# Linear attention of layer 0: one wait of TensorE moved behind the products with the carried state

## The reference, cut to what matters

```python
xn = _layernorm(x)
qkv = xn @ Wqkv + bqkv                     # split into q, k, v and 16 heads
# for every block of tokens, with a state S carried from block to block:
scores  = einsum('bhid,bhjd->bhij', qb, kb) * intra_decay
o_intra = einsum('bhij,bhjd->bhid', scores, vb)
o_inter = einsum('bhid,bhde->bhie', qb * q_decay, S)
S       = blk_decay * S + einsum('bhjd,bhje->bhde', kb * k_decay, vb)
o       = o_intra + o_inter
s = o @ Wout + bout
```

## Time and profile before

| what | value |
|---|---|
| time, median of 3 runs | 3000.16 us (2997.89 to 3001.02) |
| time of the profiled execution | 2999.55 us |
| its span, first to last instruction | 2997.8 us |
| granted TensorE clock, mean over the span | 0.984 |
| the attention of layer 0 in the span | about 0 to 574 us |
| share of the span in which PE is busy | 95% |

### The profile page before, as it was taken

The page is one execution under the profiler, slowest core; times in us unless marked ns, Lnnn a source line. Parts: engine busy times, 40 slices in busy tenths (PEclk is TensorE's granted clock), DMA queues, the critical chain, the costliest instruction groups (busy, mean ns, idle before and its releaser), DMA issues. The chain is left out here.

```text
span 2997.8 us, 54358 instructions
## 1 busy us (share of the span) xinstructions
PE 2848.9 (95%) x19392; PEld 2011.7 (67%) x19392; DVE 1857.0 (62%) x2721; ACT 1291.0 (43%) x2021; POOL 1416.7 (47%) x1003
## 2 busy tenths in 40 slices
PE   6999999799999997799999999999999789999999
PEld 5878787688888886455555555555555368888887
DVE  5656766577777764666666666666666744444444
ACT  3221111266666663355555555555555522222222
POOL 2003555122333222377777777777777732222222
PEclk9999999999999998799999999999999999999999
DMA  3221211122232224122222222222222332222221
GB/s 127 88 61 49 65 61 53 36 71 85 84 105 84 84 90 160 58 71 71 71 71 72 71 71 71 71 71 71 72 78 77 121 127 85 85 89 86 91 84 49
DMA packets 124567, 238.99 MB, mean 80 GB/s; under 512 B 13440, under 2 KB 48384, under 8 KB 124416
## 3 DMA queue, kind: packets, MB, share of 16 engines
q1 hardware_dynamic: 120896, 235.32, 23.2%
q10 hardware_dynamic: 3520, 1.46, 0.2%
HBM read 178.02 MB, written 58.72 MB: 79 GB/s over the span
## 5 line engine op out<-in xcount | busy, mean ns | idle before, releaser
L1330 DVE TENSOR_REDUCE l_attn_maxima<-l_attn_ps_max 128x2 f32<-128x1024 f32 x502 | 613.6, 1222 | 234.2 <-PE l_attn_ps_max L1455 230.2
L1301 POOL TENSOR_TENSOR l_attn_summed<-l_attn_summed,stage 128x1024 f32<-128x1024 f32 x248 | 586.0, 2397 | 52.9 <-ACT stage L1239 52.9
L1239 ACT ACTIVATE stage<-l_attn_ps_sc 128x1024 f32<-128x1024 f32 x512 | 497.8, 1029 | 157.3 <-PE l_attn_ps_sc L1443 136.0
L1301 POOL TENSOR_TENSOR l_attn_summed<-stage 128x1024 f32<-128x1024 f32 x124 | 293.4, 2388 | 240.1 <-ACT stage L1239 240.1
L1702 POOL TENSOR_TENSOR l_ffn_ht_lo<-stage,l_ffn_ht_hi 128x512 fp32r<-128x512 f32 x88 | 114.0, 1296 | 413.9 <-ACT l_ffn_ht_hi L1723 413.9
L62 PE MATMUL l_attn_ps_prep<-l_w_tile,l_x_tiles 128*128 (+1 forms) x1440 | 287.1, 348 | 6.3 <-DVE l_attn_qk_lo L1324 2.0
L62 PEld LDWEIGHTS l_attn_ps_prep<-l_w_tile,l_x_tiles 128*128 128x128 f32 x1440 | 248.9, 190 | 39.3 <-issue 29.4
L1465 PE MATMUL l_attn_ps_y<-stage,l_attn_v 128*32 128x512 f32 x2048 | 273.6, 606 | 1.1 <-ACT stage L1239 1.1
L71 PE MATMUL l_ffn_ps_fc<-l_w_tile 128*128 128x512 f32 x1024 | 268.1, 405 | 6.7 <-DVE l_w_tile L865 5.0
L71 PEld LDWEIGHTS l_ffn_ps_fc<-l_w_tile 128*128 128x128 f32 x1024 | 184.6, 190 | 41.7 <-issue 5.5
L71 PE MATMUL l_ffn_ps_out<-l_ffn_t_proj,l_ffn_ht_hi 128*128 128x512 f32 x512 | 206.9, 404 | 0.0
(11 more groups left out here) (270 smaller groups left out, 6328.6 us busy)
## 6 DMA issues: line engine op xcount, KB each, us to landing
l_x_tiles<-xt_chunks SPq DMA_DIRECT2D x160, 512.0 KB, 3.7
xt_chunks<-l_w_tile SPq DMA_DIRECT2D x32, 512.0 KB, 4.7
l_attn_xin<-in_x SPq DMA_DIRECT2D x32, 256.0 KB, 4.3
l_attn_piece<-in_w_fcT SPq DMA_DIRECT2D x16, 512.0 KB, 4.3
s<-l_attn_s_sb SPq DMA_DIRECT2D x32, 256.0 KB, 2.2
l_attn_piece<-in_w_projT SPq DMA_DIRECT2D x16, 512.0 KB, 3.9
l_ffn_xa<-in_x SPq DMA_DIRECT2D x32, 256.0 KB, 2.7
l_ffn_xb<-in_x SPq DMA_DIRECT2D x32, 256.0 KB, 2.9
```

What stands on the lines that cost most here:

```text
L1239: act.activation(probs[kt % RING][:, hs, :], ps_sc[:, hs, :], ACT.Exp, scale=ATT_SCALE).then_inc(exp_done, 1)
L1301: pool.tensor_tensor(total[:, hs, :], old[:, hs, :], probs[kt % RING][:, hs, :], ALU.add).then_inc(added, 1)
L1330: dve.tensor_reduce(maxima[b][:, j, PAIR * hp:PAIR * hp + PAIR, half:half + 1], pair, AX.X, ALU.max).then_inc(max_read, 1)
```

## The change

The wait for `masked_ready` is taken from ahead of the four products of the carried state and put behind them, just ahead of the products that read `masked`. No instruction is added or removed.

```diff
                     need(pe, zeroed, 1)
                     need(pe, state_ready, c)
                     need(pe, ot_lo_ready, c)
-                    need(pe, masked_ready, HPG * c + HPG)
                     for g in range(GROUPS):
                         pe.matmul(ps_o[:, g, :], state[q][:, g, :], q_dec[q][:, g, :], start=(g == 0), stop=False,
                                   skip_group_check=True)
+                    need(pe, masked_ready, HPG * c + HPG)
                     for g in range(GROUPS):
                         for h in range(HPG):
                             v = 2 * DIM + P * g + HD * h
```

## The result

The changed kernel takes 2989.39 us (median of 8 runs, 2987.75 to 2994.77), the one before 3000.48 (8 runs, 2997.89 to 3003.15): ratio 0.9963, 95% interval 0.9953 to 0.9972, so 8 to 14 us less. Forecast were 2991.7 us and a range of 2989 to 2997; the time lies 0.4 us inside the lower end of that range. Its profiled execution took 2989.26 us, with a span of 2987.5 us.

A forecast was written before the change was run, and what follows sets the result against it. PE, busy 95% of the span, was taken as the bound. Gains of 7.4 (ticks 15 to 29) + 1.1 (tick 1) + 0 (new wait's cost) = 8.5 us, off 3000.16, gave 2991.7 us; range 2989 to 2997.

The forecast's parts named there:

- The loss is 0.47 to 0.50 us in 15 ticks: Attention of layer 0, ticks 15 to 29: PE's stall ahead of L533 and slower L533 vanish, gaining 7.4 us in all.
- the idle time in brackets: PE's waits ahead of L533 in the profile, 6.1 us in 16 waits; said to understate the stall.
- The new wait is met 0.67 us early and costs nothing: Ahead of L538 in ticks 15 to 29, masked banks are ready 0.67 us before PE arrives; cost taken as 0.
- the rule on weight loads: At the L533 to L538 seam: TensorE may pull weight loads ahead, so a wait there could keep later loads back.
- second rival: The 15 late ticks stay at 17.1 us because something else ends last; only tick 1 gains: 2999.1 us, chance 0.12.
- first rival: The new wait costs 0.10 us in each of 32 ticks, so 5.3 us are gained: 2994.9 us, chance 0.10.
- DVE's idle time falls to 0.3 and DVE does not become the bound: Late ticks: DVE's wait for the q projection shrinks from 0.80 us to 0.3; DVE still waits for PE.
- the slower one: The wait keeps PE from holding L538's short load and matmul pairs ready: some 3007 to 3075 us, chance 0.06.
- Tick 1 gains 1.06: L533 runs inside PE's 2.70 us gap, so L538 starts at about 46.96 in place of 48.02: 1.06 us.
- The sum of 8.5: Whole kernel: 7.4 us from ticks 15 to 29, 1.1 from tick 1, 0 for the new wait's cost.
- the forecast by itself: Whole kernel: the expected case without its rivals, 2989.5 to 2994.5 us, chance 0.70.
- What made masked late: DVE in ticks with ternary work: L420 takes 1.17 us; POOL's load differs between windows, 5.27 against 27.52 us.

## Why the prediction was right, point by point

*The loss is 0.47 to 0.50 us in 15 ticks.* Right: from tick 14 to tick 30, 7.43 us were predicted and 7.43 measured, and the run with the wait moved in the loop alone has late ticks of 16.634. Going by starts and not by the idle time in brackets was the step that mattered: the brackets would have given 6.1 us for all 16 waits.

*The new wait is met 0.67 us early and costs nothing.* Right: 0.63 in the tick shown, L538 0.98 behind L532, and three further waits change nothing. The prediction says that by the rule on weight loads the sum would be nearer the second rival; a cost of the new wait in every tick is its first rival, and neither came true.

*DVE's idle time falls to 0.3 and DVE does not become the bound.* Right: 0.28, and with 0.6 us more of DVE work the late ticks still take 16.61. The second rival is out, and so is the slower one: behind the open wait of tick 1, L538 takes its 1.08 us for 32 matmuls as everywhere.

*Tick 1 gains 1.06.* It gained 1.16: I took the distance from the end of the masked banks to L533 (0.14), and L538 started 0.06 after it. The wait left in tick 1 is 1.52, where I gave about 1.7. What the step left out is the clock: behind the old wait of 2.70 it fell in one of four profiles, which cost 1.4 us more.

*The sum of 8.5.* The profiled attention gained 10.2 and the medians 11.1. What the sum lacked is tick 10 (1.64 in the pair of profiles), where the clock's dip and the landing of one load differ from execution to execution; with the load early, 9.1 are left by the medians. That the median still fell into the range, 0.4 us from its end and just below the 2989.5 to 2994.5 given for the forecast by itself, is in part luck; timed once more, the changed kernel took 2990.7, 10.0 less than before. Whether the changed kernel is on average better off in tick 10 stays open: two of its profiles have no dip, but with three more waits it had one. Behind the attention the stages varied too: the first projection of layer 1 (1183.9 and 1174.3) is 9.6 us earlier, the first of its feed-forward (2413.3 and 2401.8) 11.5, the end 10.3. So some 1 us either way of the difference belongs to no step of the change. The medians gain more than tick 1 and the late ticks do in the parts as well (3.7 against 1.2 with tick 1 alone, 8.4 against 7.4 with the loop alone, 9.6 against 7.4 with L420 moved); dips of the clock in ticks 1 and 10 of the timed runs could account for some of it, which is not shown.

*What made masked late* was named only in passing (POOL's load, and an L420 of 1.17 us). The runs show the chain: POOL's ternary operation holds up L420, L420 stands ahead of the masked banks, and these held PE.

## What to carry to other kernels

A wait belongs ahead of the first instruction that needs it: here eight matmuls of 0.98 us in all stood behind a wait of 0.37 us for data that they don't read, in 15 ticks. Read such a loss from the distances between starts in a disturbed and an undisturbed tick, since modelled matmul durations hid half of it (0.21 in brackets, 0.47 by starts). The margin that is won was room for 0.6 us more of DVE work in a tick at no cost, and a second cure at the late producer's own queue does not add to the first.

## What the runs showed of the hardware that I had not expected

A tile of 24 bytes in the middle of the allocations made matmuls of 128x512 elsewhere follow each other some 3 ns slower, and every tick 0.14 to 0.16 us longer; behind all other tiles it did not. Which of the moved tiles is the one, and what another size would do, was not tried. A fp32 tensor_scalar from SBUF to SBUF on DVE took 1.17 us in place of 0.54 when it started 0.9 before the end of a POOL operation, and ended 0.27 to 0.29 after that end wherever it had started; a bn_stats of the same tile took 0.68 in place of 0.69. After PE's waits of 2.7 to 3.2 us in tick 10 the clock stayed at 1.00 in three profiles and fell to 0.50 in the eight others that have the stall; after waits of 2.7 us in tick 1 it fell in one of four, after 3.2 in both, and after 1.5 to 2.0 in none of eight.
